# Transformer decoder layer on one core: second gate tile of the last three batches into idle PSUM banks, last expert product onto VectorE

## The reference, cut to what matters

```python
scores = jax.nn.sigmoid(x @ Wr)
_, idx = lax.top_k(scores + router_bias, TOP_K)
...
cw = jnp.zeros((T, E), dtype=x.dtype).at[jnp.arange(T)[:, None], idx].add(w)
g = jnp.einsum('th,ehi->tei', x, Wg)
u = jnp.einsum('th,ehi->tei', x, Wu)
hid = jax.nn.silu(g) * u
mlp_out = jnp.einsum('tei,eih->teh', hid, Wd)
routed = jnp.einsum('te,teh->th', cw[:, :E_MLP], mlp_out)
...
return routed + SHARED_SCALE * shared
```

## Time and profile before

| what | value |
|---|---|
| median of three executions | 180.59 us (180.39 to 182.45) |
| the profiled execution's own time | 180.98 us |
| its span, first to last instruction | 179.1 us |
| PE busy | 159.0 us, 89% of the span |
| DVE busy | 141.6 us, 79% |
| ACT busy | 126.9 us, 71% |
| POOL busy | 87.9 us, 49% |

### The profile page before, as it was taken

How to read it: one execution, slowest core, us unless ns; L and a number is a source line. 1 busy time by engine, 2 the same in 40 slices (tenths; PEclk the granted TensorE clock), 3 DMA queues, 4 the chain that set the end, 5 groups by cost and what they waited for, 6 DMA issues and landing times.

```text
span 179.1 us, 7215 instructions
## 1 busy us (share of the span) xinstructions
PE 159.0 (89%) x2682; PEld 117.8 (66%) x2682; DVE 141.6 (79%) x464; ACT 126.9 (71%) x283; POOL 87.9 (49%) x171
## 2 busy tenths in 40 slices
PE   6999497887888989999999999999799999998663
PEld 6978365564566766776788667877377668675343
DVE  2335979999976999999899899889878765868831
ACT  7266379673974768977866888847947879974670
POOL 4534667325103411356364275142744475698893
PEclk9999879999999999999999999999999999999999
DMA  5557113220332321320330133122310001010102
GB/s 133 175 207 224 40 48 96 73 60 18 93 76 49 80 66 37 91 63 9 81 91 18 38 76 78 35 62 51 77 37 29 7 6 31 2 33 0 33 0 59
DMA packets 19594, 11.11 MB, mean 62 GB/s; under 512 B 3188, under 2 KB 19188, under 8 KB 19560
## 3 DMA queue, kind: packets, MB, share of 16 engines
q1 hardware_dynamic: 19368, 10.26, 21.7%
q0 software_dynamic: 192, 0.39, 0.8%
HBM read 3.10 MB, written 1.05 MB: 23 GB/s over the span
## 4 chain that ended last, share of the span: by engine, by line
PE 62%; ACT 10%; issue 9%; DMA 6%; POOL 4%; DVE 4%; SPq 3%; ACTq 0%; POOLq 0%; DVEq 0%
PE self_bank L939 13%; PE pv_bank L939 12%; PE max_pair L939 8%; PE cross_bank L939 7%; PE soft_pair L939 7%; PE ffn_bank L939 7%; DMA bproj_all<-bproj_dram 4%; ACT probs L641 3%; PE self_bank L943 2%; SPq L363 2%; PE pv_bank L1115 2%; DMA qs<-qparts 1%; ACT hidT L711 1%; ACT vs L634 1%; DVE negmax L832 1%
## 5 line engine op out<-in xcount | busy, mean ns | idle before, releaser
L832 DVE TENSOR_REDUCE negmax<-max_pair 128x4 f32<-128x1024 f32 (+3 forms) x56 | 49.9, 915 | 6.8 <-PE max_pair L939 6.7
L641 ACT ACTIVATE probs<-soft_pair 128x1024 f32<-128x1024 f32 x40 | 41.1, 1027 | 9.8 <-PE soft_pair L939 9.3
L475 POOL TENSOR_TENSOR rstd<-vareps,exponent 128x2 f32<-128x2 f32 x24 | 17.2, 719 | 29.0 <-DVE vareps L747 28.7
L939 PE MATMUL pv_bank<-probs,vs 128*32 128x128 f32 (+3 forms) x512 | 19.0, 301 | 0.2 <-DVE x L864 0.2
L516 POOL TENSOR_TENSOR shared<-shared,tapped 128x256 f32<-128x256 f32 x24 | 17.6, 733 | 2.2 <-ACT tapped L675 1.5
L939 PEld LDWEIGHTS pv_bank<-probs,vs 128*32 128x32 f32 x512 | 13.4, 110 | 5.7 <-issue 1.8
L939 PE MATMUL max_pair<-ks,qs 64*64 64x128 bf16 (+3 forms) x512 | 15.9, 230 | 0.0
L939 PE MATMUL soft_pair<-qs,ks 64*64 64x128 bf16 (+3 forms) x512 | 15.8, 230 | 0.0
L939 PE MATMUL max_pair<-later_key,eye 64*64 64x128 bf16 (+1 forms) x224 | 11.2, 237 | 4.6 <-DMA qs<-qparts 1.4
L939 PEld LDWEIGHTS max_pair<-later_key,eye 64*64 64x64 bf16 x224 | 5.3, 105 | 11.4 <-issue 5.0
L524 POOL TENSOR_TENSOR hid<-hraw,cw 128x256 f32<-128x256 f32 x16 | 9.8, 613 | 5.4 <-DVE hraw L917 4.0
(11 more groups left out here) (182 smaller groups left out, 409.8 us busy)
## 6 DMA issues: line engine op xcount, KB each, us to landing
ks<-kparts SPq DMA_DIRECT2D x45, 64.0 KB, 2.0
qs<-qparts SPq DMA_DIRECT2D x45, 64.0 KB, 2.1
out_dram<-result SPq DMA_DIRECT2D x8, 128.0 KB, 1.9
ctxin<-ctxT_dram SPq DMA_DIRECT2D x1, 896.0 KB, 10.8
xin<-x_dram SPq DMA_DIRECT2D x1, 768.0 KB, 12.8
W<-weights_dram SPq DMA_DIRECT2D x1, 710.5 KB, 6.0
qs<-maxparts SPq DMA_DIRECT2D x32, 4.0 KB
xin<-x_dram SPq DMA_DIRECT2D x2, 128.0 KB, 2.5
```

The costliest lines, as they stand in the source:

```text
L475: nc.gpsimd.tensor_tensor(t["rstd"][b.par][:, :], t["vareps"][:, :], exponent[:, :], ALU.pow).then_inc(rstd_done[n], 1)
L641: nc.scalar.activation(probs[b.par][u][:, :, :], soft_pair[:, :].rearrange("p (r x) -> p r x", r=2), ACT.Exp).then_inc(exp_done, 1)
L832: nc.vector.tensor_reduce(negmax[:, :, first:first + n, t], of_unit(max_pair, 64 * t + 64, n, at), AX.X, ALU.max, negate=True).then_inc(ma ...
L939: return nc.tensor.matmul(out, lhsT, rhs, start=start, stop=stop, skip_group_check=True)
```

## The change

- `ffn_gate_up` of tile 1 of the batches 5, 6 and 7 writes into the banks `max_pair[:, 0:512]`, `max_pair[:, 512:1024]` and `soft_pair[:, 0:512]`. Its wait for `hraw` of tile 0 is replaced by a wait for the last reader of the scores. `tanh_g`, `gate` and `times_up` of that tile read the new bank.
- Two steps of PE and two of ACT move in `ORDER`. On PE `ffn_gate_up.6.1` goes from behind `ffn_down.5.0` to in front of `ffn_hid_t.5.0`, and `ffn_gate_up.7.1` from behind `ffn_hid_t.6.0` to in front of it. On ACT `tanh_g.6.1` goes from behind `x3T.7.0` to behind `tap.6.0`, and `tanh_g.7.1` from behind `hidT.6.0` to directly behind `tanh_g.7.0`.
- The product `hid.7.1` leaves POOL and is made on DVE (`weigh_last`), behind `times_up.7.1`, with a semaphore of its own for which `ffn_hid_t` of batch 7 waits.

```diff
+        last_hid_done = sem("last_hid_done")
...
+        def gate_bank(b, t):
+            if t == 0 or b.c < B - 3:
+                return bank_of("ffn", b)[:, :]
+            return (max_pair[:, 0:512], max_pair[:, 512:1024], soft_pair[:, 0:512])[b.c - (B - 3)]
...
-                nc.scalar.activation(tang[b.par][:, t, :], bank_of("ffn", b)[:, 0:S], ACT.Tanh, scale=0.5).then_inc(tang_done, 1)
+                nc.scalar.activation(tang[b.par][:, t, :], gate_bank(b, t)[:, 0:S], ACT.Tanh, scale=0.5).then_inc(tang_done, 1)
...
+            def weigh_last(b, t):
+                dve.wait_ge(hid0_done, b.count(2, t + 1))
+                dve.wait_ge(route, b.count(ROUTE, ROUTE))
+                dve.wait_ge(pe_hid_t, b.count(1, -1))
+                nc.vector.tensor_tensor(hid[b.par][:, t, :].rearrange("p (e i) -> p e i", e=EM),
+                                        hid0[b.par][:, t, :].rearrange("p (e i) -> p e i", e=EM),
+                                        cw[b.par][:, t, 0:EM].unsqueeze(2).to_broadcast([P, EM, I]), ALU.mult).then_inc(last_hid_done, 1)
...
             def ffn_gate_up(b, t):
                 if t == 0:
                     pe.wait_ge(tanr_done, b.count(1, 1))
+                elif b.c < B - 3:
+                    pe.wait_ge(hid0_done, b.count(2, 1))
+                elif b.c < B - 1:
+                    pe.wait_ge(max_read, PER_BATCH * B)
                 else:
-                    pe.wait_ge(hid0_done, b.count(2, 1))
-                mm(bank_of("ffn", b)[:, :], x3T[b.par][:, KC - 1 + t * P:KC - 1 + (t + 1) * P], w_gate_up).then_inc(pe_gate_up, 1)
+                    pe.wait_ge(exp_done, SOFT_N * B)
+                mm(gate_bank(b, t), x3T[b.par][:, KC - 1 + t * P:KC - 1 + (t + 1) * P], w_gate_up).then_inc(pe_gate_up, 1)
...
             def ffn_hid_t(b, _):
-                pe.wait_ge(hid_done, b.count(2, 2))
+                if b.c < B - 1:
+                    pe.wait_ge(hid_done, b.count(2, 2))
+                else:
+                    pe.wait_ge(hid_done, b.count(2, 1))
+                    pe.wait_ge(last_hid_done, 1)
```

More of the change, by code:

```diff
@@ L58 @@
         conv.6.1 sig.6.0 conv.6.2 conv.6.3 conv.7.0 skip.6.0 sig.7.0 hid.6.0 hid.6.1 skip.6.2 conv.7.1 skip.7.0 hid.7.0
-        conv.7.2 hid.7.1 conv.7.3 skip.7.2 base.6.0 base.7.0
+        conv.7.2 conv.7.3 skip.7.2 base.6.0 base.7.0
     """,
@@ L79 @@
         tanh_r.5.0 skip.4.1 exp.7.3 tanh_g.5.0 tap.5.0 exp.7.4 tap.5.1 hidT.4.0 outT.7.0 skip.5.0 skip.5.1 tap.5.2
-        relu7.5.0 x3T.6.0 tanh_g.5.1 tanh_r.6.0 o2T.7.0 tanh_g.6.0 hidT.5.0 tap.6.0 tap.6.1 tap.6.2 x3T.7.0 tanh_g.6.1
-        tanh_r.7.0 skip.6.0 tap.7.0 tanh_g.7.0 skip.6.1 relu7.6.0 tap.7.1 hidT.6.0 tanh_g.7.1 skip.7.0 tap.7.2 relu7.7.0
+        relu7.5.0 x3T.6.0 tanh_g.5.1 tanh_r.6.0 o2T.7.0 tanh_g.6.0 hidT.5.0 tap.6.0 tanh_g.6.1 tap.6.1 tap.6.2 x3T.7.0
+        tanh_r.7.0 skip.6.0 tap.7.0 tanh_g.7.0 tanh_g.7.1 skip.6.1 relu7.6.0 tap.7.1 hidT.6.0 skip.7.0 tap.7.2 relu7.7.0
         skip.7.1 hidT.7.0
@@ L113 @@
         gate.6.1 route.7.0 route.7.1 times_up.6.1 route.7.2 route.7.3 gate.7.0 times_up.7.0 route.7.4 route.7.5
-        route.7.6 route.7.7 gate.7.1 times_up.7.1 finish.6.0 finish.7.0
+        route.7.6 route.7.7 gate.7.1 times_up.7.1 hid.7.1 finish.6.0 finish.7.0
     """,
@@ L142 @@
         ffn_down.4.0 out_t.7.0 ffn_x_t.6.0 ffn_gate_up.5.1 ffn_router.6.0 o2_t.7.0 ffn_gate_up.6.0 o_proj.7.0
-        ffn_hid_t.5.0 ffn_down.5.0 ffn_gate_up.6.1 ffn_x_t.7.0 ffn_router.7.0 ffn_gate_up.7.0 ffn_hid_t.6.0
-        ffn_gate_up.7.1 ffn_down.6.0 ffn_hid_t.7.0 ffn_down.7.0
+        ffn_gate_up.6.1 ffn_hid_t.5.0 ffn_down.5.0 ffn_x_t.7.0 ffn_router.7.0 ffn_gate_up.7.0 ffn_gate_up.7.1
+        ffn_hid_t.6.0 ffn_down.6.0 ffn_hid_t.7.0 ffn_down.7.0
     """,
@@ L909, in gate @@
                     dve.wait_ge(hid0_done, b.count(2, t - 3))
-                nc.vector.scalar_tensor_tensor(out=gated[b.par][:, t, :], in0=tang[b.par][:, t, :], scalar=1.0, in1=bank_of("ffn", b)[:, 0:S],
+                nc.vector.scalar_tensor_tensor(out=gated[b.par][:, t, :], in0=tang[b.par][:, t, :], scalar=1.0, in1=gate_bank(b, t)[:, 0:S],
                                                op0=ALU.add, op1=ALU.mult).then_inc(gated_done, 1)
@@ L916, in times_up @@
                     dve.wait_ge(hid_done, b.count(2, t - 3))
-                nc.vector.scalar_tensor_tensor(out=hid0[b.par][:, t, :], in0=gated[b.par][:, t, :], scalar=0.5, in1=bank_of("ffn", b)[:, S:2 * S],
+                nc.vector.scalar_tensor_tensor(out=hid0[b.par][:, t, :], in0=gated[b.par][:, t, :], scalar=0.5, in1=gate_bank(b, t)[:, S:2 * S],
                                                op0=ALU.mult, op1=ALU.mult).then_inc(hid0_done, 1)
+            def weigh_last(b, t):
[5 more added lines that the diff above has]
+                                        cw[b.par][:, t, 0:EM].unsqueeze(2).to_broadcast([P, EM, I]), ALU.mult).then_inc(last_hid_done, 1)
             def finish(b, _):
@@ L933, in _ @@
                             "max_mid": max_mid, "div2": divide_out2, "x2": residual2, "route": choose_experts,
-                            "gate": gate, "times_up": times_up, "finish": finish})
+                            "hid": weigh_last, "gate": gate, "times_up": times_up, "finish": finish})
         @block.tensor
```

## The result

| | before | changed |
|---|---|---|
| median of 22 executions each, us | 180.48 (177.96 to 182.45) | 181.14 (179.56 to 183.62) |
| profiled execution, its span | 180.98, 179.1 | 181.48, 179.5 |

The ratio is 1.007, with a 95% interval of 1.004 to 1.010: a little slower, and within the 2% that a measurement of this kernel tells from no change. (The ratio leaves out, for each kernel, the executions over 1.5% above its fastest, so it stands further out than the two medians, which are 0.66 apart.) Predicted were 180.9 and +0.34.

What follows compares the result with a forecast made beforehand. The prediction took PE's start of hid_t.7, behind ACT's hidT.6 and down.6, as deciding the end. Batch 7's late start, +0.39, and -0.05 from the second tile gave +0.34 on 180.59, say 180.9 us; range 180.0 to 181.9.

Steps and rivals of the forecast that it cites:

- the full gain: Moved products and tanh cost others nothing, hid_t.7 starts 0.94 sooner, median 179.65; whole or partial gain had chance 0.15.
- the forecast's own case: PE decides the end; hid_t.7, down.7 and finish.7 come 0.34 later; case +0.1 to +0.5, chance 0.63.
- the rival that POOL ends last: At base.7: POOL over 0.17 later than worked out, finish.7 +0.59 to +0.92, median 181.2 to 181.5; chance 0.17.
- gate_up.6.1 ahead of hid_t.5: On PE: the product delays finish.5, whose bank ffn_x_t.7 needs; 0.39 on everything of batch 7, bounds 0 and 0.71.
- The second tile: Batch 7's early gate_up.7.1 and tanh: tang.7.1 1.17 sooner, but ACT's wait makes hidT.6 1.34 late; hid_t.7 at 173.79.
- PE's leg: Chain through hid_t.7 and down.7 on PE to finish.7: +0.34, finish.7 at 176.71 by PE.
- hid.7.1 on DVE: DVE product done by 172.8 at best, 173.35 at worst, ahead of hid_t.7 at 173.79; cost 0, hidden by down.6.
- POOL's row: POOL's list without hid.7.1, late but gapless: base.7 ends at 176.50, finish.7 at 176.54 by POOL; PE decides by 0.17.
- the first rival: At base.7: POOL ends last because DVE's hid.7.1 blocks POOL; +0.5 to +0.9, chance 0.17.
- finish.7 released by base.7: Sign of being wrong: the last step, finish.7, waiting for POOL's base.7 instead of PE; no size of its own.
- the hold: DVE's hid.7.1 comes first and holds POOL's hid.7.0 for 0.42, finish.7 +0.59; another hold of at most 0.33 gives +0.92.
- The gain arrives: At down.6 and hid_t.7: moved steps cost others little or nothing, -0.94 to -0.05, median 179.65 to 180.5; chance 0.15.

Runs made afterwards that it cites:

- e1: Changed kernel with gate_up.6.1 back behind down.5 on PE and its tanh back behind x3T.7 on ACT; finish.7 at +14.89, median 180.16 us.
- e2: Changed kernel with tanh_g.7.1 alone back behind hidT.6 on ACT; finish.7 at +14.98, median 181.00 us.
- e9: Changed kernel with hraw of batch 7, tile 1, in an idle PSUM bank, so hid.7.1 reads one SBUF operand; finish.7 at +15.14, median 181.74 us.
- e4: Changed kernel with hid.7.1 back on POOL between the last two conv steps; finish.7 at +15.74, median 181.83 us.
- e3: Changed kernel with batch 7's feed-forward in bank ffn, so it need not wait for finish.5; finish.7 at +14.88, median 179.71 us.
- e5b: Changed kernel with hid.7.1 made twice on DVE, run again after a clock drop; finish.7 at +15.69, one execution of 182.24 us.
- e7: Only the change's new banks, with every moved step and hid.7.1 at their places of before; finish.7 at +14.62, median 179.90 us.

## Why the prediction was right, and which of its terms were not

The median lies inside the stated range, but that range took in every case except the full gain, so the number says little for the sum. The shift, +0.51 in the trace and +0.66 in the medians, lies above the forecast's own case (+0.1 to +0.5) and in that of the rival that POOL ends last (+0.5 to +0.9), which had a chance of 0.17. The terms one by one:

| step, from the start of o_proj.7 | worked out | measured |
|---|---|---|
| transposes of batch 7 (before +4.38) | +4.77 | +4.80 |
| tang.7.1 (before +9.81) | +8.64 | +8.57 |
| hidT.6 (before +8.85) | +10.19 | +10.13 |
| hid_t.7 (before +11.84) | +12.24 | +12.19 |
| end of DVE's hid.7.1 | +11.25 to +11.80 | +11.74 |
| base.7's end | +14.95 | +15.24 |
| finish.7, by PE alone (before +14.82) | +15.16 | +15.11 |
| finish.7, by POOL | +14.99 | +15.33 |

**gate_up.6.1 ahead of hid_t.5** was priced at 0.39 and measured 0.42; e1, which undoes it, gives back 0.42 at the start of batch 7 and 0.44 at the end. The cause is shown; that the size came so near is luck, since two errors of 0.1 cancel. The product costs PE 0.86 from start to start at its new place (161.84 to 162.70) and not 0.96, so finish.5 starts 0.40 later (+3.82 to +4.22) and not 0.50. And the sum let ffn_x_t.7 follow finish.5 by 0.04, which it had read between other engines; it follows by 0.15 in the rows of before and in the changed kernel.

**The second tile** comes as worked out: its tanh is 1.24 sooner (1.17 worked out), hidT.6 1.28 later (1.34), hid_t.7 0.35 later (0.40) and started by PE's own queue. e2 shows that it is the tanh in ACT's list that pushes hidT.6. On PE's leg alone the forecast holds: the last matmul ends 0.29 later than before, against 0.34 forecast, and stands at the same +15.07 in e9.

**hid.7.1 on DVE** was to be held by POOL as phik is in the earlier trace rows, 0.28 behind the end, and still be hidden by down.6. It ended 0.29 behind POOL's product, and hid_t.7 didn't wait for it. The Trainium skill says in "SBUF — State Buffer", § Who interferes with whom, that of a DVE instruction with two SBUF inputs and a GpSimd instruction that reads SBUF the one that issues first blocks the other, and that DVE with at most one such input, outside its 2-port modes, doesn't contend. e9 agrees (0.42 with a PSUM operand, 0.84 without).

**POOL's row is the term that was mis-sized.** The prediction took each of POOL's instructions at 0.57 to 0.69 behind its neighbour and let base.7 end at +14.95, 0.17 ahead of what PE allows. From conv.7.2's start to the start of base.6 that made 0.69 + 0.69 + 0.68 = 2.06; measured were 175.22 - 172.80 = 2.42, 0.36 more, while POOL reached conv.7.2 0.07 sooner than worked out: 0.29 late in all. The 0.36 are two prices of the same size:

- 0.18 because conv.7.3 now stands directly behind conv.7.2. It adds to what conv.7.2 writes and waits (`shared_done`) for its end, where hid.7.1 used to stand between them. In e9, without a hold, the pair takes 1.60, so 0.87 from start to start (1.60 - 0.73). With hid.7.1 between them again, in e4, conv.7.2 hands over after 0.68 (173.84 to 174.52) and conv.7.3 shows no gap. The pair base.6 and base.7, which don't need each other, takes 1.41, so 0.68. The trace of before has the same price at an earlier place, in a row that the prediction did not read (timeline of POOL):

```profile
159.48 1.60 POOL L516 TENSOR_TENSOR shared<-shared,tapped 128x256 f32<-128x256 f32 x2
```

- 0.18 because DVE's product, itself held by POOL's hid.7.0, holds conv.7.2 in its turn: 1.78 in the changed kernel, 1.60 in e9. Where the held DVE product reached into the gap ahead of conv.7.3 (e3, and the second product of e5b), the gap of the first price hid the second one. That the gap covers it is read from the two rows and was not tried by itself.

A small term comes on top: the sum let finish.7 follow base.7 by 0.04, and it follows by 0.09 (176.63 to 176.72).

So the first rival's place, POOL's base.7, did decide the end, by 15.33 - 15.11 = 0.22, less than the 0.25 to 0.58 that the rival put on top of the forecast. finish.7 released by base.7 was named as a sign of being wrong, and in that step the prediction was: the forecast's mechanism is right for 0.29 of the 0.51, and the other 0.22 are POOL's. The rival had the hold in mind, and e9 shows that to be worth 0.19; the pair of dependent steps, half of POOL's lateness, was in neither. The rival "The gain arrives" is out for the change as made; e7 shows that its banks alone gain 0.20, but without the moves.

## What to carry to other kernels

When an instruction leaves a queue, look at the two neighbours that it leaves side by side, and take their price from a pair of the same kind in the trace and not from one instruction: here it was 0.87 instead of 0.69. The same goes for the time from one engine to the next: it was 0.04 from POOL to PE, 0.09 from POOL's base.7 to DVE and 0.15 from DVE's finish.5 to PE. A step moved forward pays in the queue it enters: the product of batch 6 filled a wait at its old place and was nearly free there, and cost all of batch 7 0.4 at its new one. An elementwise product put on DVE beside a busy POOL is half as long if one of its operands stays in PSUM (0.42 against 0.84).

## What the runs showed of the hardware that was not expected

A DVE instruction of two 128x256 operands from SBUF that met a POOL instruction of 128x256 ended 0.28 to 0.29 behind the end of that instruction: phik in the earlier trace rows, the changed kernel, e1, e2, e3 and both products of e5b. That is less than the 0.42 that it takes by itself. In the changed kernel POOL's next instruction lost 0.18 (conv.7.2), not DVE's whole 0.42. Neither figure holds for every size. In the trace of before a DVE instruction of the same kind begins 0.33 into POOL's rstd, which has only two columns, and takes its 0.42; and POOL's cskip, of two columns too, once takes 0.51 beside such an instruction, where its other seven take 0.19 to 0.20:

```profile
87.30 0.71 POOL L475 TENSOR_TENSOR rstd<-vareps,exponent 128x2 f32<-128x2 f32 x1 [1.27 <-DVE vareps L747]
87.63 0.42 DVE L772 SCALAR_TENSOR_TENSOR phiq<-expq,reluq 128x256 f32<-128x256 f32 x1 [0.41 <-ACT reluq L583]
...
105.91 0.51 POOL L539 TENSOR_TENSOR cskip<-cw 128x2 f32<-128x2 f32 x1 [1.30 <-DVE cw L901]
```

The start of o_proj.7 lies between 158.40 and 162.42 in these traces, though what stands ahead of it is the same but for the bank of one gate product. The page's row of the granted clock goes with it, in part. e7, which has 9 in every slice, starts o_proj.7 at 158.40; e4 has lower slices in its first fifth and starts it at 162.42:

```profile
PEclk9999999999999999999999999999999999999999
```

```profile
PEclk9999759999999999999999999999999999999999
```

Yet e9 has the same row as e4 and starts at 161.40, and e3 the same as e7 and starts at 159.88. e3 and e4 ran on one chip, e7 and e9 on another, and on each the start comes later where the row has lower slices; that the chip makes the rest is read off single profiles and is not shown. The executions go with the clock too: of the 31 executions of before beside e1 to e4, the median is 179.0 at a mean granted clock of 1.00, 180.4 at 0.99 and 181.0 at 0.98. Seven of e4's ten and three of e9's four stand at 0.98, and none of e3's, so the medians of the table hold the clock as well as the edit. It is why all times here are counted from o_proj.7, and why executions that differ by 1% can't settle effects of 0.2%.
